# Three edits at once: the order of the first loads and roundings, feed-forward passes that run into each other, and a gather copied in whole units

## The reference, cut to what is computed

```python
# x: [64, 64, 256]; each sequence has a type in 0..2
cond   = expert_ffn[type](x) * w0 + shared_ffn(x) * w1        # gated: gelu(x@wi0) * (x@wi1) @ wo
x      = x + attention(cond)                                  # 16 heads of 16, causal
cond2  = (expert[type](x), expert[type+1](x)) * g0 + s0(x)*g1 + s1(x)*g2 + s2(x)*g3   # relu FFNs, 1024 wide
h      = relu(relu(cond2 @ rW1 + rb1) @ rW2 + rb2)            # router
scales = softmax(h @ rW3 + rb3);  top 2 of 8 experts, 10 slots per sequence and expert
x      = x + sum(scale * (relu(slot @ eW1 + eb1) @ eW2 + eb2))
```

## Time and profile before

| | us |
|---|---|
| median of 3 runs (2357.38 to 2362.7) | 2357.82 |
| the profiled execution | 2358.76 |
| its span, first to last instruction | 2357.2 |
| TensorE matmul busy | 2284.8 (97%) |
| VectorE / ScalarE / GpSimd busy | 1140.3 / 1083.5 / 328.5 |

### The profile page before, as it was taken

How to read it: one execution, slowest core, us unless ns; L and a number is a source line. 1 busy time by engine, 2 the same in 40 slices (tenths; PEclk the granted TensorE clock), 3 DMA queues, 4 the chain that set the end, 5 groups by cost and what they waited for, 6 DMA issues and landing times.

```text
span 2357.2 us, 52378 instructions
## 1 busy us (share of the span) xinstructions
PE 2284.8 (97%) x19327; PEld 1486.6 (63%) x19328; DVE 1140.3 (48%) x2332; ACT 1083.5 (46%) x2072; POOL 328.5 (14%) x486
## 2 busy tenths in 40 slices
PE   5999999999999999999999999999999999989998
PEld 2444488887787444444445888888444444458886
DVE  5554355445998542332323444454344445444444
ACT  3554354444888442332323444443344444446663
POOL 0000000011564100000000111110000000004556
PEclk9999999999999999999999999999999999989999
DMA  4231011012444430120111333342211111012434
GB/s 126 87 104 60 28 50 36 19 33 71 107 111 89 140 107 36 54 80 28 38 42 41 117 120 116 104 139 73 77 36 37 36 36 36 36 54 74 116 98 128
DMA packets 165861, 171.94 MB, mean 73 GB/s; under 512 B 99476, under 2 KB 143508, under 8 KB 156724
## 3 DMA queue, kind: packets, MB, share of 16 engines
q1 hardware_dynamic: 138740, 80.15, 11.6%
q0 software_dynamic: 21168, 74.11, 9.5%
q10 hardware_dynamic: 5776, 15.25, 2.1%
HBM read 107.57 MB, written 50.86 MB: 67 GB/s over the span
## 4 chain that ended last, share of the span: by engine, by line
PE 94%; DVE 1%; DMA 1%; ACT 1%; issue 1%; SPq 1%; POOL 0%; ACTq 0%; POOLq 0%; DVEq 0%
PE ps L833 33%; PE ps L883 26%; PE ps L1166 14%; PE ps L1285 4%; PE ps L1297 4%; PE ps L1155 4%; PE ps L788 3%; PE ps L1016 1%; PE ps L1073 1%; PE ps L1180 1%; PE ps L1027 1%; PE ps L1064 1%; PE ps L1043 0%; DMA misc<-in_x 0%; PE ps L978 0%
## 5 line engine op out<-in xcount | busy, mean ns | idle before, releaser
L833 PE MATMUL ps<-xh,arena 128*128 (+1 forms) x5376 | 888.8, 308 | 23.4 <-DVE xh L1790 15.2
L883 PE MATMUL ps<-misc,arena 128*128 128x256 f16 (+2 forms) x4128 | 712.0, 308 | 5.9 <-DVE misc L2011 2.6
L833 PEld LDWEIGHTS ps<-xh,arena 128*128 (+1 forms) x5376 | 514.6, 98 | 292.6 <-issue 30.3
L883 PEld LDWEIGHTS ps<-misc,arena 128*128 (+1 forms) x4128 | 394.9, 98 | 218.9 <-issue 5.5
L2011 DVE SCALAR_TENSOR_TENSOR misc<-ps,misc 128x256 f16<-128x256 f32 (+1 forms) x464 | 248.1, 535 | 489.2 <-ACT misc L1421 487.3
L1421 ACT ACTIVATE misc<-ps 128x256 f16<-128x256 f32 (+1 forms) x464 | 219.0, 472 | 519.1 <-PE ps L833 518.9
L1166 PE MATMUL ps<-arena 128*128 128x512 f16 x1536 | 337.2, 379 | 0.0
L1166 PEld LDWEIGHTS ps<-arena 128*128 128x128 f16 x1536 | 148.0, 98 | 172.9
L2276 DVE TENSOR_TENSOR arena<-misc,arena 128x512 f16<-128x512 f32 x128 | 88.6, 692 | 229.2 <-ACT arena L1589 229.2
L2005 DVE TENSOR_TENSOR arena<-ps,misc 128x256 f32<-128x256 f32 (+1 forms) x200 | 101.7, 508 | 136.5 <-ACT misc L1417 135.7
L1588 ACT ACTIVATE misc<-ps,bias 128x512 f32<-128x512 f32 x128 | 87.8, 686 | 172.5 <-PE ps L1166 162.7
(11 more groups left out here) (312 smaller groups left out, 2063.0 us busy)
## 6 DMA issues: line engine op xcount, KB each, us to landing
wstage<-in_m_w POOLq DMA_DIRECT2D x16, 1024.0 KB, 5.7
parts_d<-misc POOLq DMA_DIRECT2D x64, 256.0 KB, 2.5
arena<-src_d SPq DMA_DIRECT2D x64, 256.0 KB, 3.8
src_d<-misc SPq DMA_DIRECT2D x24, 512.0 KB, 3.1
arena<-parts_d ACTq DMA_DIRECT2D x12, 1024.0 KB, 8.0
wstage<-in_c_wi POOLq DMA_DIRECT2D x6, 1024.0 KB, 5.4
wstage<-in_r_w POOLq DMA_DIRECT2D x5, 1024.0 KB, 5.5
cshare_d<-misc SPq DMA_DIRECT2D x8, 512.0 KB, 3.1
```

The source lines that it names most:

```text
L833: last = mm(ps[:, bank, col + c0:col + c0 + width], weight(p, off, half, g, wp, k * F + f * 128), xh[:, xp, k, ds(start, width)], start=(k ...
L883: last = mm(ps[:, 4 + 2 * half + m, c0:c0 + width], weight(p, off, half, 2 if p.gated else 1, wp, f * D + m * 128), hid[:, st % 4, hp, c0: ...
```

## The change

It has three parts.

*The start.* SP fetches `c_swi1` in place of `c_swo`, and ScalarE `c_swo`. POOL waits for `x_hi` (the first eight sequences rounded) before its weight fetches. ScalarE rounds the third matrix behind the first sequences. VectorE does the type tables in two pieces at steps 0 and 2 of `cs`; gate vectors and the first pair weights go from step 2 to 4, the second pair weights from 4 to 5, identities, masks and parities each one step later, `bias_scale` stays at 8.

*The passes.* In the last part of a pass TensorE issues the leading `first` products of the next (`behind(p)`), each at its place between the last `second` products, and reads the next pass's place at step 11. The last evacuate and feature of a pass move into steps 1 and 3 of the next. This is so for `cs` to `ce`, `s0` to `s1`, `s1` to `s2` and `s2` to `ee`; `ce` to attention stays.

*The gather.* A unit's sums lie in blocks of 128 columns in PSUM, and a unit is copied by one instruction of 640 elements. ScalarE has 18 units (the even ones, 5 and 7), VectorE 14; `choose(7)` and `place(7)` stand before units 9 and 13, `positions(7)` and `turn_weights(7)` behind units 8 and 15, `one_hots(7)` and `turned_weights(7)` behind 14 and 18.

```diff
+            return banks[:, :, 0:SLOTS]
...
+        XE_ACT = [u for u in range(UNITS) if u % 2 == 0 or u in (5, 7)]
+        XE_DVE = [u for u in range(UNITS) if u not in XE_ACT]
...
+        def behind(p):
+
+            return {"cs": ce, "s0": es[1], "s1": es[2], "s2": ee}.get(p.name)
...
             for j in FIRST_POOL:
                 first_x(pool, j, "x_pool")
+            pool.wait_ge(s["x_hi"], 1)
             for i in range(14):
                 fetch(i)
...
-            sp.dma_start(first_stage[2], a["c_swo"]).then_inc(s["w_first_in2"], 16)
+            sp.dma_start(first_stage[1], a["c_swi1"]).then_inc(s["w_first_in1"], 16)
...
-                prev = before(p)
-                if prev is not None:
-                    pe.wait_ge(prev.ev, prev.nev)
...
+                    elif f == 0 and prev is not None:
+                        pe.wait_ge(prev.ev, prev.nev - 1 + half)
...
+                        if st == 11 and lastone and follower is not None:
+                            pe.wait_ge(s["consts"], 1)
+                            ahead = at_chunk(follower, 0, 0)
+                            if follower.dynamic:
+                                carry(ahead)
...
+                        elif follower is not None:
+                            if nxt == n_st:
+                                pe.wait_ge(s["w_ready"], follower.need_w)
+                            first(follower, 0, nxt - n_st, ahead)
+                            if p.lead < follower.lead and st == n_st - 1:
+                                first(follower, 0, follower.lead - 1, ahead)
...
-            act.dma_start(first_stage[1], a["c_swi1"]).then_inc(s["w_first_in1"], 16)
+            act.dma_start(first_stage[2], a["c_swo"]).then_inc(s["w_first_in2"], 16)
...
-            first_weights(2)
             act.wait_ge(s["x_first0"], 48)
...
             fn(xh[:, 0, :, 256:512], xf[:, 0, :, 256:512], ACT.Copy, scale=SX).then_inc(s["x_hi"], 1)
+            first_weights(2)
...
                         if st == 1 and not first:
-                            evacuate(i - 1, 1)
+                            evacuate(p, i - 1, 1)
+                        elif st == 1 and before(p) is not None:
+                            evacuate(before(p), before(p).iters - 1, 1)
...
-                fn(xe_group(0, unit, 0), dp(unit, 0), ACT.Copy)
-                fn(xe_group(0, unit, 1), dp(unit, 1), ACT.Copy).then_inc(s["xe_hi"], 1)
+                fn(xe_group(unit), dp_slots(unit), ACT.Copy).then_inc(s["xe_hi"], 1)
...
-                v.tensor_copy(xe_group(1, unit, 0), dp(unit, 0))
-                v.tensor_copy(xe_group(1, unit, 1), dp(unit, 1)).then_inc(s["xe_lo"], 1)
+                v.tensor_copy(xe_group(unit), dp_slots(unit)).then_inc(s["xe_lo"], 1)
```

More of the change, by code:

```diff
@@ L836, in first, with at_chunk @@
                 last.then_inc(p.l1, 1)
[L838 to L857 removed]
+            def at_chunk(p, i, half):
+                if not p.dynamic:
+                    return 0, (i * 2 + half) * 512
+                c = i if p.two_experts else i * 2 + half
+                start = pe.value_load(tbl[0:1, ds(c + T_START, 1)], min_val=0, max_val=NT)
+                off = pe.value_load(tbl[0:1, ds(c + (T_OFFE if p.two_experts else T_OFFC), 1)],
+                                    min_val=0, max_val=6 * SLOT)
+                return off, start
+            def ffn(p):
+                prev, follower = before(p), behind(p)
                 def pair_place():
@@ L948, in body @@
                     return ahead
-                place0 = at_chunk(0, 0)
-                if p.dynamic:
-                    carry(place0)
-                for st in range(p.lead if p is not es[0] else 0):
-                    first(p, 0, st, place0)
+                if p is cs:
+                    pe.wait_ge(s["perm"], 1)
+                    for st in range(p.lead):
+                        first(p, 0, st, at_chunk(p, 0, 0))
                 body(0, False)
@@ L1498, in ffn @@
                 body(p.iters - 1, False, True)
[L1499 removed]
+                if behind(p) is None:
+                    evacuate(p, p.iters - 1, p.last_steps // FC - 1)
             ffn(cs)
@@ new lines, in evacuate @@
+            def evacuate(p, i, half):
+                if p.two_experts:
+                    if half == 0:
+                        return
+                    dve.wait_ge(p.l2, i * 2 + 2)
+                    dve.wait_ge(p.ev, i * 2 + 1)
+                    for c0, width in (((0, CH),) if i < NFULL else ((0, CP), (CP, CP))):
+                        last = v.scalar_tensor_tensor(outb[:, :, c0:c0 + width], ps[:, 6:8, c0:c0 + width],
+                                                      wab[:, 1, i + c0 // CP:i + c0 // CP + 1],
+                                                      outb[:, :, c0:c0 + width], ALU.mult, ALU.add)
+                    last.then_inc(p.ev, 1)
@@ new lines, in feature @@
+            def feature(p, i, half):
+                if p.dynamic and i == p.iters - 1 and (half == 1 or not p.two_experts):
+                    places = [dve.value_load(tbl[0:1, T_POS + NFULL + h:T_POS + NFULL + h + 1], min_val=0, max_val=B)
+                              for h in range(2)]
+                if p.two_experts:
+                    if half == 0:
+                        return
+                    dve.wait_ge(p.ev, i * 2 + 2)
+                else:
+                    dve.wait_ge(p.ev, (i + p.i0) * 2 + (half + 1))
+                nb = p.n // S
+                if p.dynamic and i == p.iters - 1:
+                    for h, b0 in enumerate(places):
+                        last = v.tensor_copy(gate_in[:, p.feat, :, ds(b0, nb // 2)], outb[:, :, h * CP:(h + 1) * CP:S])
+                        if h == 0:
+                            link(last)
+                    last.then_inc(p.feat_done, 1)
+                    return
+                if p.dynamic:
+                    c = i if p.two_experts else i * 2 + half
+                    b0 = dve.value_load(tbl[0:1, ds(c + T_POS, 1)], min_val=0, max_val=B)
+                else:
+                    b0 = (i * 2 + half) * nb
+                v.tensor_copy(gate_in[:, p.feat, :, ds(b0, nb)], outb[:, :, 0:p.n:S]).then_inc(p.feat_done, 1)
```

183 lines of the change are left out of this document (71 added, 112 removed).

## The result

The changed kernel takes **2342.87 us** (median of 4 runs, 2341.59 to 2344.01) where the kernel before took 2358.03 beside it (4 runs): a ratio of 0.9926, 95% interval 0.9914 to 0.9939 (the two medians as they stand give 0.9936, inside it). The forecast was 2340.4 us with 2336 to 2346 around it. The profiled execution took 2341.96 us (span 2340.4) against 2358.76 (span 2357.2): 16.8 us less, where the sum of the terms was 17.4.

The account below looks back on a forecast made before the run. TensorE, busy 97% of the span, was taken to bound the kernel. Start 4.5, passes 11.4 and gather 1.5 sum to 17.4 us, taking the profiled 2358.76 to 2341.4, or 2340.4 us as a median, range 2336 to 2346.

Parts of the forecast that it names:

- 1.3 + 0.4 + 0.8 = 2.5 us: First steps of `cs`: losses from the 24th sequence's load, the type tables at steps 0 and 2, and the moved constants.
- The late group: Start of `cs`: the 24th sequence lands at 40.9 us regardless, so TensorE stands 1.3 us before `second` of step 4.
- The constants: Steps 6 to 8 of `cs`: constants one step later meet weight quarters, VectorE lags, and TensorE stands 0.8 us.
- the rival that left the start nothing: Start: late group costs more, for instance as held-back fetches hit loads of sequences 8 to 15; 2344.9 us, chance 0.10.
- 4.3, 2.6, 4.5: Gains in us at `cs` to `ce`, at both `s0` to `s1` and `s1` to `s2`, and at `s2` to `ee`.
- the bound of 1.8 us each: Table reads at step 11: taken as 0, at worst 1.8 us for `cs` to `ce` and `s2` to `ee`.
- the clock half of that term: `s2` to `ee`: 1.7 of 4.5 us gained because the 18 products behind the hole run at the upper clock level.
- The term of 1.5: Gather: single 640-element copies and the new order of units gain 1.5 us, ends 0.3 and 2.5.
- The start keeps nearly all: Rival: the start keeps 7.0 us and the pass boundaries reach their upper end of 12; 2336.8 us, chance 0.15.
- Passes don't join: Rival where passes meet: uncovered table reads or holes elsewhere lose half of 11.4 us; 2346.1 us, chance 0.10.
- Slower by the clock: Rival in the first steps: new holes keep TensorE at its lower clock; 2371 us with eight slow steps, chance 0.04.
- sign of being wrong: A hole of 1.5 us or more in a pass's last three steps, or idle time in the second 16 steps of `cs`.

Follow-up runs that it names:

- Two copies: The changed kernel with each of the gather's 640-element copies made as two of 320 again; owners and places stay as changed: 2346.37 us (one run).
- The start alone: The kernel before with only the start part of the change, passes and gather left out: 2357.75 us (10 runs), ratio 0.9987.
- the kernel with the old owners: The changed kernel with one 640-element copy per unit, but unit owners and small-step places as before the change: 2344.99 us (one run).
- the kernel without the hold: The changed kernel without POOL's wait for `x_hi` that holds its two weight fetches back: 2345.07 us (one run).
- its repeat: The changed kernel run once more, unaltered: 2343.74 us (4 runs), ratio 0.9937.
- parities split: The changed kernel with sequences 16 to 23 rounded at step 4, gate vectors at 3, `par_mask` instructions moved to step 5: 2339.74 us, ratio 0.992.

## Why the prediction was right

**The start.** The step from 9.3 to 2.2 us for the load is confirmed in both directions: 2.2 with the fetches held back, 7 us of waiting again without (there behind SP's load). The first product came 0.3 us earlier than worked out. What went back was sized at 1.3 + 0.4 + 0.8 = 2.5 us. By TensorE's distance from step to step it was 1.7 at step 4, 0.2 at steps 1 and 5 together, 1.0 at steps 8 and 9: 2.9, less 0.3 that the first products took less. The late group was the term set too low, by 0.4. Its arrival was right (41.00 for 40.9), and so was its delivery (`second` of step 4 at 45.36 for 45.45). The place that the hole is counted from was not: the sum had this product at 44.1 without the late group, but TensorE was ready at 43.6 (39.75 and one step of 3.885), by 0.3 us because the first product came earlier and by nearly 0.3 because the first 24 took less. Whatever TensorE wins ahead of a product that comes at a fixed time is given back there in full. The kernels with this hole have that `second` at 44.9 to 45.4, whether the first product comes at 19.95 or at 20.71, beside the one whose load was late (46.42).

The constants came at the places named, 8 and 9, with 0.64 us in one row and 1.0 in sum. The term was 0.8 by a slip: by the prediction's own figures the lag at step 8 is 2.8 - 1.8 = 1.0 and not 0.8, which makes the term 1.0. As for the rival that left the start nothing, the contention did move to the loads of sequences 8 to 15, as it says: the one issued at 20.20 us takes

```profile
misc<-in_x SPq DMA_DIRECT2D x1, 64.0 KB, 7.7
```

But the last of them has landed by 29.2 us, ScalarE rounds them at 31.10 without a wait, and there is no hole at step 1.

**The passes.** 4.4, 2.7, 4.7 for 4.3, 2.6, 4.5. The end of `cs`, as rows 8:

```profile
273.14 1.47 PE L850 MATMUL ps<-xh,arena 128*128 x12
274.81 1.47 PE L894 MATMUL ps<-misc,arena 128*128 128x512 f16 x6 [0.20 <-DVE misc L2030]
276.12 2.78 PE L850 MATMUL ps<-xh,arena 128*128 x24
278.74 0.82 PE L894 MATMUL ps<-misc,arena 128*128 128x256 f16 x6
```

12 products stand in the hole ahead of the last step, 0.20 us of it is left (forecast 0.2 to 0.4, though 1.51 less 1.3 to 1.4 is 0.1 to 0.2), and the reads of the table cost nothing to be seen: the bound of 1.8 us each was not needed. Taken alone or with the others, the joint has the same 3.9 us. At the start of `ee` the rows go on without a bracket, and the clock half of that term, 1.7, was measured apart as 1.65.

**The gather.** The two durations came as worked out:

```profile
L1659 ACT ACTIVATE arena<-ps 128x640 f16<-128x640 f32 x18 | 12.0, 706 | 4.9 <-PE ps L1280 4.6
...
L2331 DVE CAST arena<-ps 128x640 f16<-128x640 f32 x14 | 11.1, 821 | 3.4 <-PE ps L1280 3.0
```

0.71 and 0.82 us. Two copies keep ScalarE busy for 14.93 us and one for 13.84, over 18 units 0.06 each, as the rows of before had it. The Trainium skill, page "ScalarE: Activation LUTs", section "What ACT_TABLE_LOAD costs", would make a copy of 640 elements 0.72 us, which agrees, and the saving 0.09, where 0.06 was measured. The term of 1.5 lies between 1.2 at equal clock and 1.8 as profiled; over all traces of the two gathers it is 2.35, because most of the new ones have the higher clock, which the term did not count. The claim that the order gives more than the copies is right by 1.1 to 0.7, as far as one execution each can tell.

**The rivals.** *The start keeps nearly all*: false, the two holes stand. *It gives nothing*: false in the whole. The start alone, measured by its runs, is worth 0.13% (0.04 to 0.23%), that is 3.1 us (0.9 to 5.4): more than nothing, and less than the rival's 7. The profiles have 4.6 to 4.7 us at the end of the first pass in both kernels, of which the start alone lost 1.7 to the clock right behind it. *Passes don't join*: false. *Slower by the clock*: in the profiled execution of the changed kernel the first pass has a clock of 1.00 with both holes in it. But the evidence against this rival was weaker than it looked: rows 2 had 1.00 around the end of `cs`, and the start alone shows 0.81 there with the same holes. Its mechanism is real in a pass: in the kernel with the old owners a hole of 3.24 us at step 4 brought the clock down and cost 1.5 us behind it. It did not spread to the next steps, so the case as a whole, with five to eight slow steps, did not come. The rule cited for this rival, in the Trainium skill, page "TensorE: Matmul & The Clock Gate", section "A second HAM failure mode: psum-queue depth-cycling", shows in attention and in the gather, where the clock swings between executions of the same instructions; no run here shows it for the small idle times of a pass (1.55 and 0.64 us).

Neither sign of being wrong appeared: the largest hole in the last three steps of a pass is 0.20 us, and the second 16 steps of `cs` have no idle time.

**What the forecast left out.** It took the profiled execution's distance to the median (0.94) for fixed, and read one execution's attention as that of all. 16.8 us between the profiles are 15.2 between the medians. The median came out 2.5 us above the forecast: 0.6 are the terms, 1.9 that the profiled execution lay 0.94 above its median before and 0.91 below it after. Of the kernel before, 34 executions have a clock on record, here and beside the experiments; by this mean clock it took on average 2362.5 us at 0.992 (11 of them), 2360.3 at 0.993 (14) and 2358.6 at 0.994 (7). The changed kernel's 8 runs, at 0.993 to 0.995, show no such slope (2341.5 to 2345.0). The range given covered this; the single number could not.

## What to carry to other kernels

Before moving the start of a kernel up, list what does not move with it: here one queue's load came at 41 us (42 in one execution) whatever was done, and it took back a quarter of 7 us until its use was put one step later. With nothing to spare, 1 us more on that one load cost the pass 3.0. Where a dependent hole ends a pass, put the next pass's independent products into it at their places, and count the clock besides the idle time: 1.7 of 4.7 us at `s2` to `ee` were the clock's. Measure a small part by the ratio of its runs to the kernel before beside them, not by the distance to a median from an earlier set of runs. Lay the granted clock beside every difference of 1 or 2 us between two profiles, before it is given a cause.

## What the hardware showed

- Small loads suffer beside large ones: with two fetches of 1 MB under way, a load of 64 KB on ScalarE's queue takes 9.3 us (6.2 in the kernel without the hold, where SP's takes 9.0), with these held back 2.2. Held back, the fetches meet the next loads, and one of these takes 7.7.
- The same 24 first products took 8.14, 7.61, 7.46 and 6.88 us in four profiles (before, changed, its repeat, parities split). They begin 0.43 us apart and end 0.22 apart; the step comes at about the fifteenth, the twelfth, the eleventh and the ninth. The granted clock of the views reads 1.00 over all of them, so here only the distances show the lower level.
- Idle time of the same length does not always lower the clock: 1.51 and 2.86 us at the end of `cs` left it at 1.00 and brought it to 0.81 in the kernel with the start alone, 3.24 us at step 4 in the kernel with the old owners to 0.72, 2.82 us before `ee` halved the speed of the products behind it, and in attention the same wait did the one or the other.
- TensorE has waits in attention of up to 2.41 us (2.24 in the changed kernel) that the profile gives to "issue". They stand at the same few places in each trace, their lengths differ, and 30 of 34 end 2.2 to 2.5 us after a 16 KB packet of the instruction queue began.
